# Second layer's loop: a pass's constants put into the banks by products with the identity on PE, not by copies on ScalarE

## The reference

```
Ax  = segment_sum(sup[:, None] * out[edge_col], edge_row, num_segments=n)
out = (x * b + (Ax + out) * a) / denom          # denom = b + normalize[:, None] * a + a
```

## Time and profile before

| | us |
|---|---|
| median of 3 runs | 3079.97 |
| lowest, highest | 3079.90, 3083.72 |
| the profiled execution's own time | 3075.2 |
| its span (first to last instruction) | 3073.4 |
| the nine passes, first gather to last product (1626.35 to 2006.38) | 380.0 |

### The profile page before, as it was taken

The page is one execution under the profiler, slowest core; times in us unless marked ns, Lnnn a source line. Parts: engine busy times, 40 slices in busy tenths (PEclk is TensorE's granted clock), DMA queues, the critical chain, the costliest instruction groups (busy, mean ns, idle before and its releaser), DMA issues.

```text
span 3073.4 us, 29956 instructions
## 1 busy us (share of the span) xinstructions
PE 2371.3 (77%) x9660; PEld 1252.1 (41%) x9660; DVE 1852.2 (60%) x3783; ACT 1326.1 (43%) x1975; POOL 1132.5 (37%) x829
## 2 busy tenths in 40 slices
PE   5779999999999547989155667618888788668877
PEld 2445555555555323545021112114444655235455
DVE  3379889898898850235744434352554646827753
ACT  2898888888874321121132323201111113255544
POOL 1363544536457614330525555610120020043322
PEclk8899999999999768999568888858888688679989
DMA  7223333333433135334634555660120020132212
GB/s 202 81 63 117 106 107 103 105 112 93 120 101 89 45 93 140 95 82 144 195 117 129 155 159 160 149 182 18 41 58 23 28 53 27 54 90 68 74 46 54
DMA packets 212761, 297.93 MB, mean 97 GB/s; under 512 B 98581, under 2 KB 98951, under 8 KB 211258
## 3 DMA queue, kind: packets, MB, share of 16 engines
q1 hardware_dynamic: 107696, 213.63, 23.3%
q0 software_dynamic: 104960, 82.99, 10.7%
HBM read 171.39 MB, written 160.48 MB: 108 GB/s over the span
## 4 chain that ended last, share of the span: by engine, by line
PE 42%; DVE 21%; issue 11%; ACT 10%; POOL 8%; DMA 6%; SPq 2%; DVEq 0%; POOLq 0%; ACTq 0%
PE bank L1792 10%; PE bank L849 5%; POOL arena L1428 5%; POOL arena L941 4%; ACT RD L416 3%; PE bank L2339 3%; PE bank L829 3%; DVE st L527 3%; PE bank L291 2%; DMA arena<-y_table,ids 2%; PE bank L292 2%; PE bank L2222 2%; DVE lst L887 2%; ACT arena L469 1%; PE bank L276 1%
## 5 line engine op out<-in xcount | busy, mean ns | idle before, releaser
L941 POOL DMA_INDIRECT arena<-x_table,idd x120 | 151.5, 1263 | 752.4 <-DVE arena L1999 188.6
L284 PE MATMUL bank<-arena 128*125 128x512 f32 x640 | 290.0, 607 | 41.3 <-DMA arena<-x_cols 23.9
L1792 PE MATMUL bank<-arena 128*125 128x512 f32 x640 | 299.7, 626 | 0.7 <-ACT arena L857 0.7
L1428 POOL DMA_INDIRECT arena<-y_table,ids x180 | 229.7, 1276 | 153.0 <-DMA y_table<-arena 100.9
L857 ACT ACTIVATE arena<-bank 128x500 f32<-128x500 f32 (+1 forms) x210 | 115.2, 589 | 383.5 <-PE bank L829 252.5
L1477 PE MATMUL bank<-arena 125*125 125x512 f32 x360 | 205.4, 702 | 96.9 <-DMA arena<-y_table,ids 94.1
L300 PE MATMUL bank<-arena 128*125 128x512 f32 x640 | 278.6, 593 | 1.3 <-ACT arena L393 1.3
L661 POOL TENSOR_TENSOR arena<-arena,rowv 125x512 f32<-125x512 f32 x80 | 106.9, 1371 | 461.3 <-PE bank L292 167.7
L1637 DVE SCALAR_TENSOR_TENSOR arena<-arena,v,bank 125x512 f32<-125x512 f32 x180 | 134.5, 747 | 205.0 <-PE bank L1477 192.3
L1529 ACT ACTIVATE bank<-arena 125x512 f32<-125x512 f32 x180 | 107.9, 601 | 272.8 <-DVE arena L1637 263.0
L849 PE MATMUL bank<-arena 128*125 128x512 f32 x480 | 210.3, 596 | 8.0 <-DVE arena L1347 8.0
(11 more groups left out here) (392 smaller groups left out, 4891.5 us busy)
## 6 DMA issues: line engine op xcount, KB each, us to landing
y_table<-arena SPq DMA_DIRECT2D x36, 896.0 KB
p_table<-arena SPq DMA_DIRECT2D x25, 896.0 KB
z_table<-arena SPq DMA_DIRECT2D x25, 896.0 KB
x_table<-arena SPq DMA_DIRECT2D x25, 896.0 KB
arena<-x_cols SPq DMA_DIRECT2D x20, 1000.0 KB, 6.1
arena<-x SPq DMA_DIRECT2D x20, 896.0 KB
out<-arena SPq DMA_DIRECT2D x20, 896.0 KB
x_by_src<-arena SPq DMA_DIRECT2D x5, 896.0 KB
```

What stands on the lines that cost most here:

```text
L284: i = nc.tensor.matmul(b[0:P, :], xT[:, k, j * P:(j + 1) * P], W1r[:, k, :], start=k == 0, stop=k == KC - 1)
L941: nc.gpsimd.indirect_dma_start(out=dst, out_offset=None, in_=table, in_offset=bass.IndirectOffsetOnAxis(ap=idx, axis=0), bounds_check=limi ...
L1428: nc.gpsimd.indirect_dma_start(out=V1[0:P, t, :], out_offset=None, in_=Yd[i % 2], in_offset=bass.IndirectOffsetOnAxis(ap=ids[:, 2, t:t + 1 ...
L1792: i = nc.tensor.matmul(b[0:P, :], fT[:, k, j * P:(j + 1) * P], W[:, k, :], start=k == 0, stop=k == KC - 1)
```

## The change

ACT's copies of the constants into the banks are removed. In their place PE multiplies the constant by the identity with `start=True`, which writes it into the bank, and then adds the tile's own product to it. The constants of tiles 0 to 3 are done at the start of a pass, that of tile t+4 right behind the own product of tile t, up to tile 19. The bank must be free, so each waits for DVE to have read the tile that was in it (`P_out`). `P_cr` is now counted by PE. The wait of an own product for its constant goes, since both are on PE and in order. ACT's wait for `M_rows` goes with its loop.

```
             def step(i):
 
+                def constant(t):
+                    pe.wait_ge(P_out, i * ET + (t - RING1 + 1))
+                    nc.tensor.matmul(bank[t % RING1][0:P, :], ident[0:P, 0:P], CR[:, t, :], start=True, stop=False,
+                                     skip_group_check=True).then_inc(P_cr, 1)
+
                 def own(t):
                     pe.wait_ge(e1_t[t], i * 16)
-                    pe.wait_ge(P_cr, i * ET + (t + 1 - ET))
                     nc.tensor.matmul(bank[t % RING1][0:P, :], Ss[:, t, :], V1[:, t, :], start=False,
                                      stop=True, skip_group_check=True).then_inc(P_sum, 1)
-
+                    if t + RING1 - 1 < ET:
+                        constant(t + RING1 - 1)
+
+                for t in range(RING1 - 1):
+                    constant(t)
                 if isinstance(i, int) and i == 1:
                     pe.wait_ge(bm_rdy, 2)
                 for g in range(EG):
...
             act.wait_ge(M_rows, 1)
 
-            def step(i):
-                for t in range(ET):
-                    act.wait_ge(P_out, i * ET + (t - RING1 + 1))
-                    nc.scalar.activation(bank[t % RING1][0:P, :], CR[:, t, :], ACT.Identity).then_inc(P_cr, 1)
-            step(1)
-            with act.Fori(2, ITERS) as i:
-                step(i)
             for g in range(EG):
                 act_root(act, c)
```

## The result

The changed kernel takes 3127.26 us (median of 4 runs, 3122.13 to 3127.94) against 3079.93 us of the kernel before on the same chip. The ratio is 1.0147, with a 95% interval of 1.0124 to 1.0170: slower by 47 us. The forecast was 3134 us in a range of 3108 to 3151.

A forecast was written before the change was run, and what follows sets the result against it. The prediction took POOL's gathers as the bound before and PE as that of the pass's middle after; 30.5 + 18 + 4 + 1.3 = 54 us more gave 3134 us, range 3108 to 3151.

The forecast's parts named there:

- ACT's copies are off the chain, gain 0: Removing ACT's 180 copies of 601 ns, which lie beside the gathers, gains 0; at most 14 us could be gained.
- A product costs 0.86 us, a group 8.07 us: On PE, a constant's product costs 0.86 us at 2.4 GHz; a group of four tiles takes 8.07 us against 6.32 of gathers.
- Four in the gap hidden: Four constants ahead of a pass's first own product take 3.4 us of PE's 7.27 us idle gap and are hidden.
- The stretch at the full clock 37.1 us, less 303.4: From first own product to L1495, nine passes of 37.1 us against 303.4 us before: 30.5 us added.
- The clock, 2.0 us a pass: PE's slow clock at a pass's start costs 2.0 us a pass, 18 us in nine, with ends 0 and 3.2.
- Rival 1: PE's clock stays full through the passes, so the 18 us term is 0: 3116 us, chance 0.17.
- The constants never wait for DVE: A constant on PE needs its bank read by DVE: 1.1 us needed, 1.72 us between, so it never waits.
- The tail, 4 us: From L1495 to the next pass's first gather, +0.5 us a pass, bounds 0 and 1.6: 4 us in eight.
- Rival 2: PE's start as slow as in the worst pass (3.2 us), every tail like pass 7's: 3153 us, chance 0.10.
- The table load, 1.3 us: ACT's table load moves from the last pass's shadow to between the first norm's variance and root: +1.3 us, once.

The follow-up runs named there:

- half_columns: The changed kernel with each constant's product on 256 of the 512 columns, the other half of the constant left out: 3077.06 us, ratio to before 0.9992.
- pe_gap_only: Against the kernel before, PE makes only the constants of tiles 0 to 3, ACT copies the other 16: 3081.64 us, ratio 1.0006.
- pe_all_but_gap: Against the changed kernel, ACT makes the constants of tiles 0 to 3, PE those of tiles 4 to 19: 3124.05 us, ratio to before 1.0148.
- after_fill: The changed kernel with four more products, results unused, behind the four constants in PE's idle gap: 3114.41 us, ratio to before 1.0115.
- pe_three_of_four: Against the kernel before, PE makes the constants of the first three tiles of each group, ACT the fourth's: 3118.78 us, ratio 1.0132.
- before_split: The kernel before with the store of tiles 12 to 15 issued in two pieces, 12-13 and 14-15: 3090.34 us, ratio 1.0038.

## Why the prediction was right, step by step

- **ACT's copies are off the chain, gain 0.** Right. With none of them (half_columns) the ratio to before is 0.9992 [0.9977, 1.0006].
- **A product costs 0.86 us, a group 8.07 us.** Measured: 0.86 and 8.06. Halving the columns halves the price of a product.
- **Four in the gap hidden.** Right, shown by pe_gap_only and pe_all_but_gap.
- **The stretch at the full clock 37.1 us, less 303.4.** Nearly right. With the clock held up the passes took 37.3 to 37.6, 37.4 in the mean of seven, so this term was about 3 us too low in nine passes.
- **The clock, 2.0 us a pass.** Somewhat too high. The mean over the nine stretches of 8 us is 0.75, which is 2.0 us by the prediction's reckoning, but after_fill gives back only 1.5 in each of seven passes. Clock and products together were forecast as 351.9 us for nine passes and came to 351.3. That they fit so well is in part luck, since one was too high by about what the other was too low. The way to the clock's term was in part wrong too: I let the loss depend on the idle gap's length, and pe_all_but_gap had the longer gap and the same loss. Rival 1, with the rule of the Trainium skill's "TensorE: Matmul & The Clock Gate" ("HAM oscillation — how this bites in real kernels"), gave a full clock at the start. The stretches at 0.67 to 0.79 are against that reading here, with about 4 us idle to 43 us of products without a gap. The section also warns of idle gaps by their own length alone, and read so it doesn't speak for rival 1.
- **The constants never wait for DVE.** Right in the changed kernel. The trace puts eight waits of a constant's weight load down to DVE, 0.85 us each, all at a pass's very start, ahead of the idle gap, and PE's products have none. pe_three_of_four shows it from the other side.
- **The tail, 4 us.** Too high: 1.8. The piece of tiles 12-15 was issued 4.6 us ahead of L1503 (1808.77 to 1813.37), as forecast. That of 16-17 came 2.57 us behind it and was held 1.05 us in the fourth pass:

```profile
1808.77 0.31 SPq L1187 DMA_DIRECT2D y_table<-arena  x1
...
1811.34 0.31 SPq L1187 DMA_DIRECT2D y_table<-arena  x1
1811.69 1.05 SPq L1188 DMA_DIRECT2D y_table<-arena  x1
```

  Tails were 4.9 to 5.2. Rival 2 took the distance to L1495 alone for what counts, but at the same distance the spacing of the two pieces decides. Pass 7 of the kernel before had 4.5 us of distance, 1.72 of spacing and a tail of 6.3. Where they are 3.75 us apart (1741.30 to 1745.05 in the kernel before) the tail is 4.3. The distance counts as well: with the same spacing of 1.72 us and as long a hold, the tail is 5.7 us at 5.0 us of distance (pass 6 of pe_gap_only) and 6.7 to 7.0 at 3.7 us.
- **The table load, 1.3 us.** Right, 1.34 us (1.54 against 0.20).
- **Missed:** the last pass's first rows came 7.4 us behind the gather's start, before 5.4, which is 2 us of the 53. That the tail was forecast about 2 us too high makes up for it, which is luck again.

On the profiled executions the sum of 54 us stands against 52.7. The medians differ by 47, and the interval of the ratio is 38 to 52 us, so the sum is a little too high against the medians. The profiled execution of the kernel before was 4.8 us faster than its median, and that of the changed kernel was the slowest of its four.

## What to carry to other kernels

Before work is moved from an idle engine to a busy one, work out the busy engine's time for one unit of the pipeline against the pace of what feeds it. Up to that pace the work is free, and above it every microsecond counts, and also those that waiting used to hide, such as a slow clock at the start. A change of one stage's rhythm also changes how stores bunch up at the end of a pass; that was worth 16 us in two of these kernels. And when the last user of an engine ahead of a wait is taken away, look for what had been hidden behind it: here a table load.

## What the runs showed that I had not expected

- SP's issue of a store of 250 rows is held for 2.1 to 2.3 us when it comes 1.7 us behind a store of 500 rows, for 1.05 to 1.2 us at 2.6 us, and not at 3.75 us. What stands behind it on SP waits too, small as it is.
- Whether PE was idle for 4 or for 7.5 us ahead of a pass made no difference to its loss at the start (351.3 and 350.6 us in nine passes), while keeping it busy did.
- Splitting the store cut the tails to 4.3 to 4.7 us and lengthened the passes by more (before_split: -3.6 us and +13.7).
